# A row region per expert, a row buffer per tile, six weight sets, and batch 0 routed ahead of batch 1's second norm

## The reference

```python
x = x + norm(attention(norm(x)))      # causal, 16 heads, a bias by distance, logits / 64
x = x + norm(moe(norm(x)))
# moe, for each of the N = 2048 tokens xf:
shared = gelu(xf @ Wfc_s + bfc_s) @ Wproj_s + bproj_s          # 128 -> 512 -> 128
topk_p, topk_i = top_k(softmax(xf @ Wr), 2)                    # 2 of 8 experts
topk_p = topk_p / sum(topk_p)
routed = sum over the two e: (gelu(xf @ Wfc[e] + bfc[e]) @ Wproj[e] + bproj[e]) * gate[e]
return shared + routed
```

## Time and profile before

| | us |
|---|---|
| median of 3 runs (909.36 to 913.86) | 909.73 |
| the profiled execution | 905.23 |
| its span, first to last instruction | 903.1 |
| busy: TensorE | 702.7 (78%) |
| busy: VectorE | 622.8 (69%) |
| busy: ScalarE | 553.8 (61%) |
| busy: GpSimd | 324.9 (36%) |

### The profile page before, as it was taken

One profiled execution on the slowest core, in us unless ns is written; L12 is line 12 of the kernel. 1 busy time (PEld: TensorE's weight loads), 2 busy tenths in 40 slices (PEclk: granted clock), 3 DMA queues, 4 the chain that ended last, 5 costly groups with the idle time before them and its releaser, 6 DMA issues.

```text
span 903.1 us, 16620 instructions
## 1 busy us (share of the span) xinstructions
PE 702.7 (78%) x4325; PEld 619.2 (69%) x4325; DVE 622.8 (69%) x1632; ACT 553.8 (61%) x1304; POOL 324.9 (36%) x384
## 2 busy tenths in 40 slices
PE   3828999999999999999999999936821565664640
PEld 2626888888888888888888888834621555654630
DVE  5516888888988888888888888886810433343437
ACT  2316887887888878888788887827410433342322
POOL 1307853333324434334333342343175122222141
PEclk9978999999999999999999999977965888787675
DMA  7796543534544355354353444200132354545434
GB/s 263 256 281 107 130 116 79 130 93 93 116 106 103 93 116 127 65 134 104 81 128 93 99 110 114 73 1 1 67 129 74 110 167 151 173 156 176 164 94 122
DMA packets 88671, 108.29 MB, mean 120 GB/s; under 512 B 47840, under 2 KB 68576, under 8 KB 86208
## 3 DMA queue, kind: packets, MB, share of 16 engines
q1 hardware_dynamic: 74048, 99.13, 41.2%
q10 hardware_dynamic: 12096, 3.65, 2.6%
q0 software_dynamic: 2496, 5.15, 1.6%
HBM read 48.32 MB, written 26.03 MB: 82 GB/s over the span
## 4 chain that ended last, share of the span: by engine, by line
PE 64%; DMA 11%; issue 9%; DVE 7%; POOL 3%; ACT 2%; SPq 2%; ACTq 2%; DVEq 0%; POOLq 0%
PE out_ps L1377 15%; PE score_ps L1344 15%; PE trans_ps L1359 14%; PE shared_ps L1391 6%; DMA k_hl<-split_scratch 3%; DMA y_scratch<-normed_rows,wqk 2%; PE shared_ps L1260 2%; PE score_ps L1260 2%; PE shared_ps L1261 2%; PE shared_ps L1262 2%; DMA q_hl<-split_scratch 2%; ACTq L752 2%; POOL y_scratch L678 1%; PE score_ps L1262 1%; PE score_ps L1261 1%
## 5 line engine op out<-in xcount | busy, mean ns | idle before, releaser
L761 ACT ACTIVATE probs<-score_ps,row_min 128x128 f32<-128x128 f32 (+7 forms) x256 | 190.1, 743 | 65.8 <-DVE row_min L1001 51.5
L1014 DVE TENSOR_TENSOR pT_lo<-trans_ps,pT_hi 128x512 fp32r<-128x512 f32 (+3 forms) x384 | 201.6, 552 | 17.9 <-ACT pT_hi L782 17.8
L782 ACT ACTIVATE pT_hi<-trans_ps 128x512 fp32r<-128x512 f32 (+3 forms) x384 | 185.4, 492 | 43.6 <-PE trans_ps L1359 31.8
L1001 DVE CUSTOM_DVE_ANT_0 score_ps<-score_ps,bias 128x128 f32<-128x128 f32 (+7 forms) x256 | 194.6, 760 | 24.7 <-PE score_ps L1344 21.3
L1359 PE MATMUL trans_ps<-ident,probs 128*128 128x128 f32 x1152 | 191.2, 275 | 2.3 <-DVE pT_lo L1014 1.9
L1344 PE MATMUL score_ps<-k_hl,q_hl 128*128 128x512 f32 (+2 forms) x768 | 184.0, 353 | 5.0 <-DMA k_hl<-k_hl 3.8
L579 POOL TENSOR_TENSOR acc<-acc,head_out 128x512 f32<-128x512 f32 x64 | 82.8, 1293 | 213.6 <-DVE head_out L1032 213.5
L1377 PE MATMUL out_ps<-pT_hi,v_hl 128*128 128x512 f32 (+2 forms) x384 | 156.7, 409 | 1.1 <-DVE pT_lo L1014 1.1
L1359 PEld LDWEIGHTS trans_ps<-ident,probs 128*128 128x128 f32 x1152 | 137.9, 141 | 26.5 <-DVE pT_lo L1014 11.9
L1344 PEld LDWEIGHTS score_ps<-k_hl,q_hl 128*128 128x128 f32 x768 | 135.7, 190 | 25.6 <-DMA k_hl<-k_hl 4.0
L1377 PE MATMUL out_ps<-pT_lo,v_hl 128*128 128x512 f32 (+2 forms) x384 | 133.3, 347 | 0.0
(11 more groups left out here) (183 smaller groups left out, 1197.9 us busy)
## 6 DMA issues: line engine op xcount, KB each, us to landing
q_hl<-k_hl SPq DMA_DIRECT2D x64, 256.0 KB, 3.7
k_hl<-k_hl SPq DMA_DIRECT2D x32, 512.0 KB, 4.3
k_hl<-split_scratch SPq DMA_DIRECT2D x32, 512.0 KB
v_scratch<-probs SPq DMA_DIRECT2D x16, 512.0 KB, 4.1
v_raw<-v_scratch SPq DMA_DIRECT2D x32, 256.0 KB, 4.6
split_scratch<-normed_rows SPq DMA_DIRECT2D x16, 512.0 KB, 5.6
q_hl<-split_scratch SPq DMA_DIRECT2D x14, 512.0 KB
normed_rows<-in_W_halves SPq DMA_DIRECT2D x16, 256.0 KB, 5.9
```

The lines of the kernel that those rows point to most:

```text
L761: act.activation(probs[s % 4][:, 0:n], scores_of(s % QB)[:, 0:n], ACT.Exp, bias=row_min[:, s:s + 1], scale=-1.0, accum_out=row_sum[:, s:s ...
L782: act.activation(pT_hi[c][:, CH * g:CH * g + m, q * P:(q + 1) * P], trans_ps[k % 2][:, 0:m * P].rearrange("p (m q) -> p m q", q=P), ACT.Co ...
L1001: dve.tensor_tensor_reduce(out=ps, in0=ps, in1=bias_b[b][:, T - n:T], scale=1.0, scalar=3e38, op0=ALU.add, op1=ALU.min, accum_out=row_min[ ...
L1014: dve.tensor_tensor(pT_lo[c][dst], trans_ps[k % 2][:, 0:m * P].rearrange("p (m q) -> p m q", q=P), pT_hi[c][dst], ALU.subtract).then_inc(p ...
```

## The change

1. **Rows.** `rows_scratch` becomes one region of 2048 rows (`RE`) for each of the 8 experts, and grows from 5888 to 18432 rows. A token's row is now `2048 * expert + rank`, so it needs no count of other tokens' totals. The table of tiles gets the first row of each tile (`tile_base`), which SyncE reads into a register for each row load.
2. **Empty rows.** Their content is made by GpSimd (`make_empty`) in the memory of `wv` and in a part of `normed_rows`; each head stores 9 x 128 of them (`store_empty`, two DMAs on SyncE after `store_half`), and GpSimd moves the numbers on for the next head (`move_empty`). ScalarE's two DMAs are gone. ScalarE's first normalisation after attention waits for all of these stores, and so do the scatters.
3. **Routing by batch.** Logits, choice, ranks and slots are done for batch 0 before batch 1's `add_normed` on VectorE. The first 8 scatters of batch 0 stand on GpSimd ahead of `root(2, QB, NB)`, the other 8 behind it. The table of tiles is made after batch 1's slots. The shared expert's splits on VectorE stand behind all of it.
4. **Buffers.** Six weight sets instead of three: the new ones lie in the memory of `pT_lo`, `nT_hi` and `nT_lo`. A row buffer for each of the 23 tiles, and a bias for each tile. A load of weights waits for the result of the tile six before, a load of rows only for the turned rows of that tile, no more for a stored result. The low parts of the shared expert's weights move to `pT_hi`.
5. **Tiles.** On all three engines `tile_in(i + 1)` stands ahead of `tile_units(i)`.
6. **End.** GpSimd adds the two results of each token (`sum_parts`), VectorE does one add where it did two.
7. **Fillers.** At the start TensorE does 40 and 28 transposes of the identity that nobody reads (`keep_busy`).

The core of the diff (operations that only take a slice per batch are left out):

```diff
     HI_OF_TILE = 2
-    NR = 6
+    NW = 6
+    RE = B * T
+    EA, EB = 7, 2
+    ROWS = H * P * (EA + EB)
+    assert ROWS >= (E - 1) * RE + (NT - RE // TS) * TS
...
-        tile_rows = [flat(wqk[:])[:, i * NJ * ROW:(i + 1) * NJ * ROW].rearrange("p (j r) -> p j r", r=ROW) for i in range(NR)]
+        halves = lambda a: [a[:, 0:2 * HID], a[:, 2 * HID:4 * HID]]
+        tile_w = [halves(flat(k_hl[0][:])), halves(flat(k_hl[1][:])), [q_hl[0][:], q_hl[1][:]],
+                  halves(flat(pT_lo[0][:])), halves(nT_hi[:]), halves(nT_lo[:])]
+        tile_bias = sb("tile_bias", [P, NT, 8])
+        rows_in = lambda a, i: a[:, i * NJ * ROW:(i + 1) * NJ * ROW].rearrange("p (j r) -> p j r", r=ROW)
+        in_wqk, in_bias = H * 2 * DH // (NJ * ROW), H * 2 * P // (NJ * ROW)
+        tile_rows = ([rows_in(flat(wqk[:]), i) for i in range(in_wqk)] + [rows_in(flat(bias_all[:]), i) for i in range(in_bias)]
+                     + [rows_in(flat(normed_rows[:]), 2 + i) for i in range(NT - in_wqk - in_bias)])
+        empty_a = wv[:, 0:EA * ROW].rearrange("p (j r) -> p j r", r=ROW)
+        empty_b = flat(normed_rows[:])[:, 3 * HID:3 * HID + EB * ROW].rearrange("p (j r) -> p j r", r=ROW)
...
+            def store_empty(h):
+
+                sp.wait_ge(empty_moved, h + 1)
+                for rows_of, lo, n in ((empty_a, 0, EA), (empty_b, H * P * EA, EB)):
+                    sp.dma_start(bass.AP(rows_dram.tensor, lo * ROW + h * (P * n * ROW), [[n * ROW, P], [1, n * ROW]]),
+                                 rows_of.rearrange("p j r -> p (j r)")).then_inc(rows_emptied, 16)
+
...
                 e = sp.value_load(tile_expert_i[0:1, i:i + 1], min_val=0, max_val=E - 1)
-                if i >= 3:
-                    sp.wait_ge(yT_ready, i - 2)
+                if i >= NW:
+                    sp.wait_ge(yT_ready, i - NW + 1)
+                elif i == NW - 2:
+                    sp.wait_ge(fc_psum, NCH * HB)
                 for part in range(2):
-                    sp.dma_start(tile_w[i % 3][part].bitcast(f32),
+                    sp.dma_start(tile_w[i % NW][part].bitcast(f32),
                                  bass.AP(split_dram.tensor, e * (2 * P * 2 * HID) + part * (P * 2 * HID),
-                                         [[2 * HID, P], [1, 2 * HID]])).then_inc(tile_w_loaded[i % 3], 16)
-                sp.dma_start(tile_bias[i % 3][:], bass.AP(W_bias.tensor, e * (P * 8), [[8, P], [1, 8]]))\
-                  .then_inc(tile_bias_loaded[i % 3], 16)
+                                         [[2 * HID, P], [1, 2 * HID]])).then_inc(tile_w_loaded[i % NW], 16)
+                sp.dma_start(tile_bias[:, i, :], bass.AP(W_bias.tensor, e * (P * 8), [[8, P], [1, 8]]))\
+                  .then_inc(tile_bias_loaded[i % NW], 16)
 
             def load_rows(i):
 
-                if i >= NR:
-                    sp.wait_ge(y_stored[(i - NR) % 2], 16 * NJ * ((i - NR) // 2 + 1))
-                sp.dma_start(tile_rows[i % NR], rows_dram[i * TS:(i + 1) * TS, :].rearrange("(j p) r -> p j r", p=P))\
-                  .then_inc(tile_rows_loaded[i % NR], 16)
+                first_row = sp.value_load(tile_base_i[0:1, i:i + 1], min_val=0, max_val=ROWS - TS)
+                if i >= NW:
+                    sp.wait_ge(xT_psum, i - NW + 1)
+                sp.dma_start(tile_rows[i], bass.AP(rows_dram.tensor, first_row * ROW, [[ROW, P], [P * ROW, NJ], [1, ROW]]))\
+                  .then_inc(tile_rows_loaded[i % NW], 16)
 
             sp.wait_ge(half_stored, 16 * HALVES)
             sp.wait_ge(scores_ready, H * S)
+            sp.wait_ge(oT_psum, H * B * NC)
             sp.wait_ge(table_ready, 1)
-            for i in range(3):
+            for i in range(NW - 2):
                 load_weights(i)
             sp.wait_ge(dispatched, 16 * 2 * NB)
-            for i in range(NR):
+            for i in range(NW - 2):
                 load_rows(i)
-            for i in range(3, NT):
+            for i in range(NW - 2, NT):
                 load_weights(i)
-                if i + NR - 3 < NT:
-                    load_rows(i + NR - 3)
+                load_rows(i)
...
+            def make_empty():
+
+                pool.wait_ge(wv_split, 1)
+                for rows_of, lo, n in ((empty_a, 0, EA), (empty_b, H * P * EA, EB)):
+                    then_wait(pool.memset(rows_of, 0.0))
+                    then_wait(pool.iota(empty_dest[:, 0:n], pattern=[[1, n]], base=2 * B * T + lo, channel_multiplier=n))
+                    then_wait(pool.tensor_copy(rows_of[:, :, D + 1].bitcast(i32), empty_dest[:, 0:n]))
+
+            def move_empty(h):
+
+                if isinstance(h, int) and h == 0:
+                    pool.sem_inc(empty_moved, 1)
+                    return
+                pool.wait_ge(rows_emptied, h * 32)
+                pool.sem_inc(pool_passed, 1)
+                for rows_of, n in ((empty_a, EA), (empty_b, EB)):
+                    dest = rows_of[:, :, D + 1].bitcast(i32)
+                    last = pool.tensor_scalar(dest, dest, P * n, None, ALU.add)
+                last.then_inc(empty_moved, 1)
 
...
+            def dispatch(b, picks):
+
+                pool.wait_ge(slots_ready, b + 1)
+                pool.wait_ge(fields_ready, b + 1)
+                pool.wait_ge(rows_emptied, 32 * H)
+                for i in picks:
+                    for t in range(QB * b, QB * (b + 1)):
                         pool.indirect_dma_start(rows_dram, bass.IndirectOffsetOnAxis(slot_u[i][:, t:t + 1], 0),
                                                 rows[i][:, t, :], None).then_inc(dispatched, 16)
 
...
+            dispatch(0, [0])
             root(2, QB, NB)
-            copy_rows(0)
+            dispatch(0, [1])
             copy_rows(1)
-            dispatch()
+            dispatch(1, [0, 1])
             for i in range(NT):
                 store_tile(i)
+
+            def sum_parts(c):
+
+                part = slice(CH * c, CH * (c + 1))
+                pool.wait_ge(y_loaded[c], 32)
+                pool.tensor_tensor(y_part[0][:, part, :], y_part[0][:, part, :], y_part[1][:, part, :], ALU.add).then_inc(y_summed, 1)
+
+            sum_parts(0)
+            sum_parts(1)
             for c in range(NCH):
                 root(3, CH * c, CH * (c + 1))
+                if c + 2 < NCH:
...
                 copy_v(t)
-            act.wait_ge(empty_ready, 1)
-            act.dma_start(bass.AP(rows_dram.tensor, 0, [[ROW, P], [P * ROW, NT * NJ], [1, D + 1]]),
-                          empty_row[:].unsqueeze(1).broadcast_to([P, NT * NJ, D + 1])).then_inc(rows_emptied, 16)
-            act.dma_start(bass.AP(rows_dram.tensor, D + 1, [[ROW, P], [P * ROW, NT * NJ]]),
-                          empty_dest[:].bitcast(f32), allow_slow_non_contiguous=True).then_inc(rows_emptied, 16)
...
+            def find_slots(b):
+
+                blocks = slice(QB * b, QB * (b + 1))
+                dve.wait_ge(rank_psum, b + 1)
+                then_wait(dve.scalar_tensor_tensor(
+                    out=place[:, blocks, :], in0=count[:, 0:E].unsqueeze(1).broadcast_to([P, QB, E]), scalar=float(RE),
+                    in1=shared_ps[:, QB * b * E:QB * (b + 1) * E].rearrange("p (t e) -> p t e", e=E), op0=ALU.mult, op1=ALU.add))
+                for i in range(2):
+                    then_wait(dve.tensor_tensor(place_of[:, blocks, :], place[:, blocks, :], pick[i][:, blocks, :], ALU.mult))
+                    then_wait(dve.tensor_reduce(slot_f[i][:, blocks], place_of[:, blocks, :], AX, ALU.add))
+                    last = dve.tensor_copy(slot_u[i][:, blocks], slot_f[i][:, blocks])
+                last.then_inc(slots_ready, 1)
+
...
+            scale_and_offset(2, 0, QB)
+            dve.wait_ge(acc_added, H * B * NC)
+            moments(acc, QB, NB)
+            make_order()
+            for c in range(NC):
+                nT_evac(1, c)
+            take_logits(0)
+            choose(0)
+            find_slots(0)
+            add_normed(1)
+            scale_and_offset(2, QB, NB)
+            for c in range(NC, NCH):
+                nT_evac(1, c)
+            take_logits(1)
+            choose(1)
+            find_slots(1)
+            find_tiles()
+
...
             transposes(0, 0)
+            keep_busy(40)
             transposes(0, 1)
             for t in range(4):
                 values_of_all(t)
+                if t == 3:
+                    keep_busy(28)
                 if t % 2:
                     transposes(0, 2 + t // 2)
...
             pe.wait_ge(wo_scaled, H * B * NC)
+            pe.wait_ge(nT_ready, NCH + NC)
+            logits(0)
             pe.wait_ge(wfc_ready, 1)
-            for c in range(NC):
-                pe.wait_ge(nT_ready, NCH + c + 1)
-                hidden_units(0, c, 0)
+            hidden_units(0, 0, 0)
+            ranks(0)
+            hidden_units(0, 1, 0)
             for c in range(NC, NCH):
                 transposes(1, c)
             pe.wait_ge(nT_ready, 2 * NCH)
-            logits()
+            logits(1)
```

(2 more changed lines are left out.)

234 lines of the change are left out of this document (121 added, 113 removed).

## The result

| | before | after |
|---|---|---|
| median (us) | 910.96 (4 runs, 909.36 to 913.86) | 796.06 (4 runs, 794.4 to 797.9) |
| the profiled execution, its span | 905.23, 903.1 | 796.33, 794.3 |
| mean granted clock | 0.897 | 0.942 |

The ratio of the times is 0.8736, with a 95% interval of 0.8704 to 0.8768. The prediction was 802, range 784 to 831, faster with 0.97.

The account below looks back on a forecast made before the run. Nothing is full: a circle of waits (result store, weight load, TensorE) bounds the tile stage. Start -11.5, routing -11.5, tiles -83.6 and end -0.5 sum to -107: 798 from the profiled run, 803 from the median; forecast 802, range 784 to 831.

Parts of the forecast that it names:

- Tiles, -83.6: Tile stage: no wait for result stores, six weight sets in flight; 22 steps of 3.75 us instead of 7.55, -83.6 us.
- The clock: Tile stage: with TensorE busy 3.3 of 3.75 us, the granted clock should keep its full level instead of 0.78.
- the first rival: Tile stage: clock or DMA engines hold it at about 5.0 us a tile, 27.5 us more, 829; chance 0.15.
- Start, -11.5: Before attention: without ScalarE's flood of empty rows, V's load lands at 60.1 instead of 71.62, all attention 11.5 us earlier.
- ScalarE's hole: Start: ScalarE spends 50.50 to 64.60 us issuing one DMA of single destination numbers; no term of its own.
- Head loop, 0: Loop over heads: SyncE's extra stores of empty rows, 0.6 MB per head, cost 0; at most 24 us.
- Routing, -11.5: Routing by batch, from batch 0's transposed input: first tile starts at 686 instead of 697.54, -11.5 us; bounds -16 and -5.
- The shared route: Routing: the shared expert's work, behind all routing on VectorE, ends last by 3 us, at 686 against the scatters' 683.0.
- End, -0.5: After the tiles: VectorE loses four adds of 0.69, GpSimd's sums stand ahead of each norm; -0.5 us, between -3 and +2.
- A start that keeps its hole: Second rival, start: V loads crawl for another reason, 8 us back, 810, or 814 with nothing gained; chance 0.10.
- Slow scatters: Third rival, routing: scatters slow beside VectorE, 24 at 1.51 us cost 13 us, 815; chance 0.12.
- Slower stores: Fourth rival, tile stage: GpSimd's result-store pairs take 8.6 us instead of 2.5, slower than before, 915; chance 0.03.

Follow-up runs that it names:

- the flood alone: Changed kernel with only the first of ScalarE's old DMAs added back (3 MB in rows of 512 bytes, into memory of its own): 821.04 us, one run.
- no_fill: Changed kernel without the 40 and 28 filler transposes that nobody reads: 805.93 us, ratio 0.8861 to the kernel before.
- act_block: Changed kernel with 46 copies of 128x128 on ScalarE (about 14 us, results unused) where its two DMAs stood, no traffic: 816.63 us, one run.
- out4: Changed kernel with four result buffers instead of two: 788.06 us, ratio 0.8641 to the kernel before.
- sets3: Changed kernel with three weight sets instead of six, row buffers still one for each tile: 819.63 us, ratio 0.8979 to the kernel before.
- sets3_rows6: Changed kernel with three weight sets, and row loads that wait for the stored result of the tile six before: 878.37 us, one run.
- in_behind: Changed kernel with the next tile's input behind a tile's first products on TensorE, ScalarE and VectorE: 817.50 us, ratio 0.8964 to the kernel before.
- scat4: Changed kernel with four scatters of batch 0 ahead of batch 1's root instead of eight, twelve behind it: 800.10 us, ratio 0.8784 to the kernel before.
- rows6: Changed kernel with six weight sets, and row loads that wait for the stored result of the tile six before: 827.27 us, one run.
- early: Changed kernel with the shared expert's first two blocks worked on in the holes of batch 1's routing: 795.71 us, ratio 0.8731 to the kernel before.
- best: Changed kernel with four result buffers, four scatters ahead of the root and the shared expert's early blocks together: 785.68 us, ratio 0.8616 to the kernel before.

## Why the prediction was right

**Tiles, -83.6 against -84.9.** The step "SyncE no longer waits for a result store before it can ask for the next weights, and six sets are in flight" is shown: to undo either costs 26 to 28 us in the stage (24 by the median of the three sets), to undo both brings back 7.42 us a step. The reordering of the input is the third part, 23 us, and shows only when the circle is gone. The value of 3.75 us a tile was right for a wrong reason at one point. I had "3.3 while the lead of six sets lasts, then near 4.0 at the DMA engines"; what held the later steps was the two result buffers, and with four of them it is 3.30 at the same DMA load. So 3.75 came near 3.69 in part by luck: one wait stood in for another. Two single steps, 4.83 and 5.01 us, lie over the 4.5 that was named as a sign of being wrong. The row with the 2.23 us landing stood at the head of the rows; I asked who no longer waits for it, and not who else does.

**The clock.** The granted clock was 1.00 as forecast, and the first rival (5.0 us a tile) did not come. From 700 to 740 us it was 0.78 with three sets and the old wait, TensorE busy 59%; 0.87 with three sets alone, at 76%; and 1.00 with the input behind the products, at 73%. So the busy share does not order them. The first had 22.4 us of waits for weights from 676 to 740, the second 13.4, the third none for weights (17.9 us of others, 1.3 on average). The Trainium skill (TensorE: Matmul & The Clock Gate, section "HAM oscillation") says that a loop which waits for a DMA in each round can start each round slow. The three traces agree; in the changed kernel there is no such wait left.

**Start, -11.5 against -15.0.** The step that "the flood delays V's load, and what hangs on it" is shown by the flood alone. The mis-sized term is the sum for V's landing: 50.9 + 4.2 + 0.4 + 4.6 = 60.1, measured 55.87. The last store was issued at 48.3 instead of 50.9, and the load took 3.2 us from issue to cast instead of 5.0. The sum had put the fillers at 0; without them V's load is issued 1.0 to 2.2 us later (no_fill), so they are a part of the 4.2 us. I also took ScalarE's hole for a side matter; by itself it holds the start 10.9 us back (act_block), which the forecast did not need, since both went.

**Head loop, 0.** From the second head's first product to batch 0's turned input 529.3 us before and 529.9 after. The stores of empty rows cost nothing that shows.

**Routing, -11.5 against -8.4.** Counted from batch 0's turned input, the steps came out as worked out: first scatter at 11.3 (forecast 11.1), root of batch 1 at 21.5 (21.9), its turned input at 29.7 (31.1), the first second-layer product at 50.1 (50.0), the last scatter's end at 65.9 (64.3). (Three links of the recorded sum are 0.3 to 0.5 us longer than their own terms: 613.33 + 2.7 is 616.0, 624.4 + 10.3 is 634.7, 656.5 + 20.6 is 677.1. None changes which route is last.) The shared route was last, as forecast, but by more: TensorE needed 21.3 us from there to the turning instead of 18.6. I had priced its low clock at 2 us; the 14 products up to 654.5 us ran at 0.43 each instead of 0.23, 2.9, and a wait of 1.48 was not in the sum. Tile 0 came at 75.8 instead of 72.7. That it stood at 674.08 us of the span, where 674 was forecast, is luck: the start was 3.5 us better and routing 3.1 worse.

**End, -0.5 against -0.4.** As forecast.

**The sum.** The span fell by 108.8 us, 107 were forecast, so the terms explain 1.7 of the 6 us between 802 and 796. The rest is the step to the median: I had kept the 4.5 us by which it stood above the profiled execution, and in the changed kernel the two agree (796.06, 796.33).

**The other rivals.** A start that keeps its hole did not come: V's cast is 15.75 us earlier. Slow scatters: the 16 on the path took (662.79 - 642.87)/15 = 1.33 us each with their gap instead of 1.29, the longest 1.46 beside VectorE's splits; 24 x 0.04 = 1 us, not 13. Slower stores: GpSimd's pairs took 2.2 to 2.5 us and never stood in the way by their own length; it was their landing.

**What stays open.** Tile 0 starts 9.9 us after the last scatter in the changed kernel and 8.6 to 9.7 in out4, sets3, sets3_rows6 and in_behind, but 14.4 in scat4, 15.8 in no_fill, 16.3 in rows6 and over 17 in the three kernels with ScalarE's DMAs or copies. There, and in early and best, ScalarE, VectorE or both stand still for 3 us and more in the shared part although by the records what they need has been computed. SyncE's first weight loads run at that time, yet they do in the kernels without the stall too. In best and early SyncE is slow as well: its first four weight loads, which wait for nothing, go out from 639.6 to 659.7 us in best, and from 646.4 to 654.5 in the changed kernel. rows6 differs from the changed kernel in nothing before that point but what SyncE will wait for later, so that wait cannot be the cause. No run tells what is. The verdicts on scat4, early and no_fill are therefore drawn from the stretches, and not from the whole time; whether leaving out the fillers brings on the stall of no_fill is not shown either way.

## What to carry to other kernels

When a wait disappears, list every other wait for the same event before you price what is left: here the store's landing only changed whom it holds, and two more buffers of 1 KB a partition gave 8 us more. Count a pipeline's lead in time and not in tiles: from a tile's first product to its stored result it was 23 us, six steps, so "six tiles back" was no reserve. Where two circles bind together, undoing each alone shows a third of the gain each, and only both together show all of it.
